# Splitting the row maxima before the transposition instead of behind it

## What is computed

```python
xn = layernorm(x)
q, k, v = bitnet_linear(xn, ...)            # weights reduced to their signs, scaled per output channel
# 32 query heads and 8 key/value heads of 32 columns: 4 query heads share a key head
scores = einsum('bhqd,bhkd->bhqk', q, k) / sqrt(32)
out = einsum('bhqk,bhkd->bhqd', softmax(scores), v)
attention = bitnet_linear(out, o_weight, o_scale)
ffn = (silu(xn @ gate) * (xn @ up)) @ down  # 4-bit weights, dequantised in groups of 128 rows
result = x + attention + ffn
```

## Time and profile before

| | |
|---|---|
| median of 3 runs | 2633.19 us |
| the profiled execution | 2632.85 us, its span 2630.8 us |
| mean granted TensorE clock | 0.972 |
| busy: PE, DVE, ACT, POOL | 92%, 70%, 57%, 37% of the span |
| attention (first unit's `top_max` to the last one's) | 337.8 to 1243.9 us of the span |

### The profile page before, as it was taken

One profiled execution on the slowest core, in us unless ns is written; L12 is line 12 of the kernel. 1 busy time (PEld: TensorE's weight loads), 2 busy tenths in 40 slices (PEclk: granted clock), 3 DMA queues, 4 the chain that ended last, 5 costly groups with the idle time before them and its releaser, 6 DMA issues.

```text
span 2630.8 us, 33118 instructions
## 1 busy us (share of the span) xinstructions
PE 2427.1 (92%) x12408; PEld 948.7 (36%) x12408; DVE 1840.8 (70%) x2362; ACT 1498.5 (57%) x1476; POOL 982.5 (37%) x545
## 2 busy tenths in 40 slices
PE   2399899999999999999589999999999999999998
PEld 1344322222222222222234444444444444444444
DVE  6756677777677677676154777777777777777777
ACT  3533246666666666666412666666666566666664
POOL 1000047878888788779600112122000112122000
PEclk9799889999999999999799999999999999999999
DMA  5100035455545454455412101112111311112211
GB/s 165 64 4 33 22 73 79 75 81 79 78 72 79 75 77 74 76 85 69 103 68 92 33 32 49 33 46 98 41 41 64 129 33 48 33 48 101 100 41 64
DMA packets 173706, 174.61 MB, mean 66 GB/s; under 512 B 87586, under 2 KB 119202, under 8 KB 173558
## 3 DMA queue, kind: packets, MB, share of 16 engines
q1 hardware_dynamic: 111286, 150.62, 18.1%
q0 software_dynamic: 62272, 22.03, 11.0%
HBM read 160.08 MB, written 65.45 MB: 86 GB/s over the span
## 4 chain that ended last, share of the span: by engine, by line
PE 79%; DVE 9%; issue 4%; POOL 4%; ACT 2%; DMA 1%; SPq 1%; DVEq 0%; ACTq 0%; POOLq 0%
PE ps L1307 29%; PE ps L1323 15%; PE ps L1212 8%; PE ps L1184 8%; PE ps L1160 6%; DVE zone L934 6%; PE ps L1287 4%; PE ps L1200 4%; PE ps L1224 4%; POOL zone L504 3%; POOL dequantised L525 1%; DVE zone L812 1%; ACT zone L656 1%; PE ps L1339 0%; DMA zone<-in_L_attn_o_weight_dram 0%
## 5 line engine op out<-in xcount | busy, mean ns | idle before, releaser
L934 DVE TENSOR_REDUCE zone<-ps 128x1 f32<-128x512 f32 x1024 | 652.0, 685 | 258.2 <-PE ps L1184 255.9
L1307 PE MATMUL ps<-xT,zone 128*128 128x512 f16 x3584 | 774.6, 379 | 3.6 <-DVE zone L1098 2.8
L656 ACT ACTIVATE zone<-ps,sm 128x1024 f32<-128x1024 f32 x512 | 565.3, 1113 | 315.5 <-PE ps L1200 229.6
L504 POOL TENSOR_TENSOR zone<-zone 128x1024 f32<-128x1024 f32 x256 | 632.3, 2580 | 103.2 <-PE ps L1224 58.0
L1075 DVE TENSOR_SCALAR ps<-ps,zone_c 128x1024 f32<-128x1024 f32 x392 | 506.8, 1293 | 161.1 <-PE ps L1307 159.1
L725 ACT ACTIVATE ps<-ps,zone_c 128x1024 f32<-128x1024 f32 x392 | 426.5, 1088 | 261.4 <-PE ps L1307 259.6
L1307 PEld LDWEIGHTS ps<-xT,zone 128*128 128x128 f16 x3584 | 350.2, 98 | 427.3 <-DVE zone L1098 4.2
L1184 PE MATMUL ps<-zone 96*128 96x512 f16 x1024 | 405.4, 397 | 47.6 <-DMA zone<-zone 10.6
L1323 PE MATMUL ps<-zone 128*128 128x512 f16 x1792 | 387.1, 379 | 0.0
L1086 DVE TENSOR_SCALAR ps<-ps,zone_c 128x1024 f32<-128x1024 f32 x216 | 279.3, 1293 | 93.0 <-PE ps L1323 92.8
L555 POOL CAST zone<-zone 128x1024 f16<-128x1024 f32 x56 | 58.0, 1036 | 725.2 <-DVE zone L1079 725.2
(11 more groups left out here) (127 smaller groups left out, 1276.3 us busy)
## 6 DMA issues: line engine op xcount, KB each, us to landing
zone<-dequantised SPq DMA_DIRECT2D x84, 512.0 KB, 3.6
dequantised<-zero_points SPq DMA_DIRECT2D x84, 256.0 KB, 4.3
zone<-zone SPq DMA_DIRECT2D x384, 32.0 KB, 2.3
zone<-_attn_hidden_states_dram SPq DMA_DIRECT2D x16, 512.0 KB, 6.7
zone<-inverse_sums SPq DMA_DIRECT2D x128, 64.0 KB, 2.1
attention<-zone SPq DMA_DIRECT2D x32, 256.0 KB, 2.0
xT<-attention SPq DMA_DIRECT2D x4, 2048.0 KB, 12.0
dequantised<-in_L_ffn_gate_w_dram POOLq DMA_DIRECT2D x28, 256.0 KB, 6.2
```

What stands on the lines that cost most here:

```text
L504: nc.gpsimd.tensor_tensor(duo[n % 3], prob[:, e % 8, :], prob[:, (e + 2) % 8, :], add).then_inc(s["sum_ok"], 1)
L656: A(prob[:, e % 8, :].rearrange("p (a c) -> p a c", a=2), ps[:, 2 + 2 * (e % 2):4 + 2 * (e % 2), :], ACT.Exp, scale=gam[:, 0:1]).then_inc( ...
L934: V.tensor_reduce(mxs[:, u % 2, half, i % 16:i % 16 + 1], ps[:, half, :], AX, amax).then_inc(s["max_ok"], 1)
L1307: last = MM(ps[:, 4 * s2 + 2 * m + c, :], ring[:, buf, m * H + g * P:m * H + (g + 1) * P], xT[:, hf, part, g, c * 512:(c + 1) * 512], star ...
```

## The change

The split into a high part and a rest is made on the 128 x 16 maxima in SBUF, ahead of the transposition. `top_max` becomes `split_max` with three dependent instructions, `split_rows` becomes `copy_rows` with one. The transposition now takes 32 columns of float16 (high parts in columns 0 to 15, rests in 16 to 31) in place of 16 of float32. `mrow` lies in 32 partitions in place of 16, and further on in `zone_c`. The view `zst` is defined and not used. Number and size of the DMAs are the same.

```diff
-        mtop = zone_d[:, 64:80]
+        mhl = zone_d[:, 64:80].bitcast(f16)
...
-        mrow = zone_c[0:16, 0:256].bitcast(f16).rearrange("p (n h c) -> p n h c", n=2, h=2)
+        zst = zone_c[:, 0:512].bitcast(f16).rearrange("p (n c) -> p n c", n=2)
+        mrow = zone_c[:, 512:640].bitcast(f16).rearrange("p (n c) -> p n c", n=2)
...
                 for part in range(2):
                     sp.dma_start(qst[96 + part:97 + part, u % 3, :, :].rearrange("a h (q c) -> a (h q) c", q=4),
-                                 mrow[:, u % 2, part, :]).then_inc(s[f"m_in{u % 3}"], 16)
+                                 mrow[16 * part:16 * part + 16, u % 2, :]).then_inc(s[f"m_in{u % 3}"], 16)
...
-            def top_max(u):
+            def split_max(u):
                 dve.wait_ge(s["max_ok"], 32 * u + 32)
-                V.tensor_reduce(mtop, mxs[:, u % 2, :, :].rearrange("p h c -> p c h"), AX, amax).then_inc(s["top_ok"], 1)
-
-            def split_rows(u):
+                m = mxs[:, u % 2, 0, :]
+                ch.inc(V.tensor_tensor(m, m, mxs[:, u % 2, 1, :], amax))
+                settle()
+                ch.inc(V.tensor_scalar(mhl[:, 0:16], m, -1.0 / MU, None, mult))
+                settle()
+                V.scalar_tensor_tensor(mhl[:, 16:32], m, -1.0 / MU, mhl[:, 0:16], mult, sub).then_inc(s["mhl_ok"], 1)
+
+            def copy_rows(u):
                 dve.wait_ge(s["m_pe"], u + 1)
-                m = ps[0:16, 7, 0:P]
-                ch.inc(V.tensor_scalar(mrow[:, u % 2, 0, :], m, -1.0 / MU, None, mult))
-                settle()
-                V.scalar_tensor_tensor(mrow[:, u % 2, 1, :], m, -1.0 / MU, mrow[:, u % 2, 0, :], mult, sub).then_inc(s["mrow_ok"], 1)
+                V.tensor_copy(mrow[0:32, u % 2, :], ps[0:32, 7, 0:64].bitcast(f16)).then_inc(s["mrow_ok"], 1)
...
             def maxima_rows(u):
-                pe.wait_ge(s["top_ok"], u + 1)
+                pe.wait_ge(s["mhl_ok"], u + 1)
                 if u >= 2:
                     pe.wait_ge(s["evd_ok"], u - 1)
-                TR(ps[0:16, 7, 0:P], mtop, id32[:]).then_inc(s["m_pe"], 1)
+                TR(ps[0:32, 7, 0:64].bitcast(f16), mhl[:, 0:32], id16[:]).then_inc(s["m_pe"], 1)
```

More of the change, by code:

```diff
@@ L223, in layer_kernel @@
             kv_out q_in0 q_in1 q_in2 m_in0 m_in1 m_in2 k_in0 k_in1 v_in0 v_in1 const_ok
-            s_pe max_ok top_ok m_pe mrow_ok st_pe exp_ok pv_pe dn_pe sum_ok ev_ok evd_ok
+            s_pe max_ok mhl_ok m_pe mrow_ok st_pe exp_ok pv_pe dn_pe sum_ok ev_ok evd_ok
             dc_in0 dc_in1 rc_ok rs_out rb_in0 rb_in1 mu_ok oh_ok ol_ok
@@ L930, in row_max @@
                 if i % 16 == 0 and u >= 2:
-                    dve.wait_ge(s["top_ok"], u - 1)
+                    dve.wait_ge(s["mhl_ok"], u - 1)
                 for half in range(2):
@@ L953, in _ @@
                 if i == 15:
-                    top_max(0)
+                    split_max(0)
                 if i == 17:
-                    split_rows(0)
+                    copy_rows(0)
             for e in range(STEPS):
@@ L961, in _ @@
                 if k == 6 and u + 1 < UNITS:
-                    top_max(u + 1)
+                    split_max(u + 1)
                 if k == 7 and u + 1 < UNITS:
-                    split_rows(u + 1)
+                    copy_rows(u + 1)
                 if k == 12 and u:
```

## The result

The changed kernel takes 2818.31 us (median of 4 runs, 2809.23 to 2826.05), the kernel before beside it 2633.02 (4 runs, 2632.19 to 2639.95). The ratio is 1.0696, with a 95% interval of 1.066 to 1.0733: 185 us slower, where the prediction said 56 and at most 79. The profiled execution took 2822.97 us, 190.1 more than that of before. Of these, 184.1 us lie between the first and the last unit's row maxima (340.1 to 1430.3 us, where it was 337.8 to 1243.9); the rest of the program takes 6 us more.

The account below looks back on a forecast made before the run. TensorE, holding 79% of the chain that ended last, was taken as the bound. Waits of 74.4 us less 16.9 hidden gave 57.5, and 2632.85 + 57.5 = 2690.4; the forecast was 2689 us, range 2645 to 2712.

Parts of the forecast that it names:

- The lengths alone cost nothing: Before step 7's first row maximum: three dependent instructions take 0.53 us, inside the 0.64 us available, so worth 0.
- Two inputs in SBUF, and the short `tensor_scalar`, wait for GpSimd; an input of PSUM or a reduction doesn't: All three new VectorE instructions (L940, L942, L944) wait for GpSimd's running instruction; what they replace never did; chance 0.60.
- One, two or three waits, each until a running `add_pair` ends: Behind `top_max`, per unit: one wait in 8 units (14.5 us), two in 9 (27.9), three in 6 (32.0); sum 74.4.
- The unit of rows 3: Attention unit with `top_max` at 391.93 us: one wait, row maximum 1.81 us late, unit about 30.5 us long.
- that of rows 7: Attention unit where L940 waits until 449.82 and L942 until about 452.3: two waits, row maximum 2.7 us late.
- the six units with three waits: Attention units where all three new instructions wait in turn: 4.6 to 6.7 us each, together 32.0 us.
- None, because a DMA issue of GpSimd keeps `add_pair` off: Behind `top_max` in 8 units: no wait, as an issue keeps `add_pair` off for 0.6 us or nothing runs; 0 us.
- up to 2.5 us: Sign: records of L940, L942 and L944 last 0.17 us beside an issue, up to 2.5 elsewhere, each ending with an `add_pair`.
- at most three deep: Between steps 7 and 8: GpSimd's pair (1, 1) needs step 8's sums, so a wait spans at most three.
- 16.9 us of it hidden by waits for GpSimd that were there anyway: In units where TensorE already waits for GpSimd, existing excess hides 16.9 of the 74.4 us of waits, leaving 57.5.
- The pattern of GpSimd against the steps repeats: In attention, GpSimd's place in a unit, set by `divide` waiting 28 times for its DMA (103.7 us), stays under the change.
- The unit of rows 8 takes 33.6 us: Attention unit with late `divide`: row maximum 4.9 us late, only 0.9 of it new on 32.68, so about 33.6 us.

Follow-up runs that it names:

- The PSUM version: The changed kernel with the unit's maxima reduced into PSUM in place of SBUF, so each new instruction has at most one SBUF input: 2637.0 us, ratio 0.9995.
- The stalls of fixed length: The kernel before with an unused reduction of 2048 or 4096 columns behind `top_max`: 2686.07 us (ratio 1.0188) and 2788.91 us (ratio 1.058).

## Why the prediction was wrong

The direction was right, and so was the mechanism where no DMA issue is near. The time was not: 2689 with a top of 2712, against 2818. Step by step:

- *The lengths alone cost nothing*: right. The PSUM version has three dependent instructions at the same place, the same transposition and copy, and the time of the kernel before.
- *Two inputs in SBUF, and the short `tensor_scalar`, wait for GpSimd; an input of PSUM or a reduction doesn't*: right, each shown by a run.
- *One, two or three waits, each until a running `add_pair` ends*: right where no issue is near. The unit of rows 3 took 30.30 us against a forecast of 30.5, that of rows 7 was 2.5 us late against 2.7, and the six units with three waits had 28.0 us against 32.0. In the ten units with no issue in the waits the delays sum to 36.9 us.
- *"None, because a DMA issue of GpSimd keeps `add_pair` off", 8 units at nothing*: this step failed. They cost 38.3 us: one 0.1, the others 4.8 to 6.0 each. Issues also lengthened units in the neighbouring kinds: the seven with one wait 31.1 us against 12.6, the nine with two 40.0 against 27.8. With the six of three waits that makes 137.3 us over 30 units, not 74.4 over 31. All of the excess lies in the 19 units with an issue in the waits, or just ahead of the `add_pair` at work: some 100 us, where the forecast had at most 74.4 - 32.0 = 42.4. I took the issue for a gap in GpSimd's use of SBUF. The runs show that an instruction which becomes ready in it, with `add_pair` queued behind, waits through the issue and one or two of these. For the same reason "up to 2.5 us" was wrong as the length of one record; "at most three deep" held, counted in `add_pair`. The reading of the rows was wrong too. The 0.6 us of rows 9 hold for that unit, but in four of the eight (`top_max` at 567.10, 653.89, 1099.90 and 1186.38 us in the kernel before) the next `add_pair` starts 0.15 to 0.34 us behind `top_max`, ahead of L944's 0.41, so even by the prediction's own rule these were not free.
- *No term for TensorE's clock*: the second failure, 66.9 us. The prediction foresaw that TensorE idles 1.5 to 4 us between steps 7 and 8, and priced that as idle time alone. The stalls of fixed length show the price behind it: nothing in most units at 1.78 us, 1.56 at 3.91. The Trainium skill ("TensorE: Matmul & The Clock Gate", section "What's actually happening") says that the slow clock is the default and that activity releases the full one. The trace agrees in kind: 1.94 us for eight matmuls behind the stall of 5.5 us, 1.07 ahead of it. I had not applied it to stalls of a few us.
- *16.9 us of it hidden by waits for GpSimd that were there anyway*: about right, 20.5.
- *The pattern of GpSimd against the steps repeats*: right. In 25 of the 30 units the `add_pair` at `top_max` stands within 0.3 us of its place before, and `divide`'s wait for its DMA is 107.7 us in 28 times, against 103.7 in rows 10.
- *The unit of rows 8 takes 33.6 us*: it took 33.67, but by chance. The sum was 0.9 us of new delay on an excess of 4.0; what happened is 3.0 us of delay and 2.0 more with a lower clock.

In one line: 74.4 - 16.9 = +57.5 was the forecast, 137.3 + 66.9 - 20.5 = +183.7 the measurement. About half of the gap is the clock's term; the other half is delay, in the units with an issue. Taking the issues away does not give back that half in full: the delays fall from 137.3 to 102.0 us, and the clock's term to 50.3, because GpSimd then stands elsewhere against the steps.

Two things stay open. Why an issue lets the following `add_pair` go ahead of a VectorE instruction whose record starts earlier isn't visible: the trace shows starts and ends, not who asked first. And the clock's term is a remainder in the changed kernel; TensorE's busy time supports its sum, but its size a unit (1.5 to 3.1 us) does not follow the delay. Three units that are 2.4 to 2.5 us late have 2.8 to 2.9 us more, twice what the fixed stall of 3.91 us has, and two units of the run without issues that are just as late have none.

## What to carry to other kernels

Before small VectorE work is moved into SBUF on a critical path, count its SBUF inputs and look at what GpSimd does then: 0.17 us became up to 6.0, and the same steps with the maxima in PSUM cost nothing. A DMA issue in GpSimd's queue is no gap if a long instruction is ready behind it. A stall of TensorE has a second price in its clock: here 1.56 us a unit on top of a delay of 3.91, mostly none on top of 1.78, and 2.9 or none on top of 2.4; look at the granted clock of the stretch behind each stall, not at its idle time alone.

## What was not expected of the hardware

- One VectorE instruction of 16 columns stood for 5.83 and 6.00 us across a GpSimd DMA issue and two `add_pair`, whose records last 5.3 us together; across an issue with nothing ready behind it, 0.17 us (a `tensor_scalar`: 0.37 and 0.47). Without the issue no hold was over 2.37 us.
- A `tensor_scalar` of 16 float32 columns to float16 is held as long as a two-input one (52.3 against 52.8 us over 32 units).
- Taking GpSimd's DMA issues (84) out of attention is worth 23 us to the kernel before, and moving one DMA ahead of others on the sync engine's queue 23 us as well. Each of the two removes the same excess.
- TensorE idled for 2.0 us in two units of one run; behind one the clock fell and the unit took 2.86 us longer, behind the other it stayed up.
